# Right sides in 64x64 tiles with a block-diagonal state of two heads, moved by four transfers

## What is computed

```python
k = l2norm(silu(x @ Wk)); q = silu(x @ Wq); v = silu(x @ Wv)
beta = sigmoid(x @ Wbeta) * 2.0; log_f = log_sigmoid(x @ Wf1 @ Wf2)
# per step, two updates of the state S[b, h, key, value]:
bS = einsum('bhk,bhkv->bhv', b_t, S)
S = exp(g)[..., None] * S + a_t[..., None] * bS[:, :, None, :] + k_t[..., None] * v_t[:, :, None, :]
o = einsum('bhk,bhkv->bhv', q_t, S)
# then: y = rms_norm_per_head(o * sigmoid(gate)) * norm_w @ Wo
# x = layernorm(x + y); x = layernorm(x + x @ (W + lora).T + b)
```

## Time and profile before

| | us |
|---|---|
| median of 3 runs | 2623.15 (2622.76 to 2631.74) |
| span of the profiled execution, first to last instruction | 2622.0 |
| TensorE matmul busy | 2288.4 (87%) |
| TensorE weight load busy | 1721.9 (66%) |
| VectorE busy | 1601.7 (61%) |
| ScalarE busy | 1618.0 (62%) |
| GpSimd busy | 458.8 (17%) |
| matmuls of right_sides (L733), busy | 362.2 |
| mean granted clock of TensorE | 0.950 |

### The profile page before, as it was taken

One profiled execution on the slowest core, in us unless ns is written; L12 is line 12 of the kernel. 1 busy time (PEld: TensorE's weight loads), 2 busy tenths in 40 slices (PEclk: granted clock), 3 DMA queues, 4 the chain that ended last, 5 costly groups with the idle time before them and its releaser, 6 DMA issues.

```text
span 2622.0 us, 225147 instructions
## 1 busy us (share of the span) xinstructions
PE 2288.4 (87%) x102472; PEld 1721.9 (66%) x102472; DVE 1601.7 (61%) x3940; ACT 1618.0 (62%) x3048; POOL 458.8 (17%) x555
## 2 busy tenths in 40 slices
PE   6788898999988899998999998989999988999785
PEld 2556666666666666666676666666666666766573
DVE  2456366666556676656666665666666566666533
ACT  3556466666666666656666666666666666666543
POOL 1011111111111111111111111111111111111210
PEclk7879899999999999999999999999999999999987
DMA  3244455534555554455554455555445555534541
GB/s 95 74 110 121 110 148 148 141 104 127 145 141 151 137 141 111 132 138 146 144 137 118 124 145 146 148 141 142 113 129 143 145 148 148 136 103 132 140 125 41
DMA packets 692934, 338.90 MB, mean 129 GB/s; under 512 B 551794, under 2 KB 651728, under 8 KB 692816
## 3 DMA queue, kind: packets, MB, share of 16 engines
q1 hardware_dynamic: 692816, 337.67, 48.2%
HBM read 35.57 MB, written 16.78 MB: 20 GB/s over the span
## 4 chain that ended last, share of the span: by engine, by line
PE 86%; issue 10%; DVE 2%; ACT 1%; DMA 1%; SPq 0%; ACTq 0%; DVEq 0%
PE bank L570 14%; PE bank L733 13%; PE bank L712 11%; PE bank L704 8%; PE bank L724 7%; PE bank L716 5%; PE bank L593 5%; PE bank L683 5%; PE bank L622 5%; PE bank L643 3%; PE bank L577 3%; PE bank L694 2%; PE bank L602 2%; PE bank L587 2%; PE bank L584 2%
## 5 line engine op out<-in xcount | busy, mean ns | idle before, releaser
L473 POOL TENSOR_TENSOR state<-moved,edge 128x512 f32<-128x512 f32 x252 | 292.3, 1160 | 1821.9 <-DVE moved L1093 1821.9
L712 PE MATMUL bank<-parts,w_now 32*32 32x64 f32 x16512 | 420.1, 223 | 4.8 <-DMA w_now<-w_row 3.6
L570 PE MATMUL bank<-x_col,w_kqv 128*128 128x512 f32 x768 | 370.6, 619 | 48.5 <-issue 47.9
L856 ACT ACTIVATE parts<-bank,cf 128x256 f32<-128x256 f32 x512 | 214.6, 470 | 319.5 <-DVE o_col L1087 310.7
L716 PE MATMUL bank<-aq_now,delta 32*32 32x16 f32 x16512 | 403.7, 179 | 9.2 <-issue 9.2
L716 PEld LDWEIGHTS bank<-aq_now,delta 32*32 32x32 f32 x16512 | 391.7, 110 | 6.7 <-issue 6.7
L712 PEld LDWEIGHTS bank<-parts,w_now 32*32 32x32 f32 x16512 | 377.2, 110 | 17.1 <-issue 5.0
L733 PE MATMUL bank<-uq_now,s_now 32*32 32x24 f32 x32768 | 362.2, 189 | 14.5 <-issue 14.4
L733 PEld LDWEIGHTS bank<-uq_now,s_now 32*32 32x32 f32 x32768 | 337.1, 107 | 24.1 <-issue 18.2
L1116 DVE COPY_PREDICATED aq<-ci,bank 128x128 f32<-128x128 int32 x256 | 77.1, 301 | 410.3 <-PE bank L704 276.7
L1087 DVE TENSOR_TENSOR o_col<-qs,bank 128x64 f32<-128x64 f32 x512 | 89.5, 216 | 388.6 <-PE bank L716 384.7
(11 more groups left out here) (99 smaller groups left out, 3814.1 us busy)
## 6 DMA issues: line engine op xcount, KB each, us to landing
s_now<-state SPq DMA_DIRECT2D x256, 256.0 KB
uq_now<-uqv SPq DMA_DIRECT2D x256, 192.0 KB
t_now<-t_t SPq DMA_DIRECT2D x256, 128.0 KB, 2.0
w_now<-w_row SPq DMA_DIRECT2D x256, 128.0 KB
uq_a<-uqv SPq DMA_DIRECT2D x64, 384.0 KB
low<-uqv SPq DMA_DIRECT2D x64, 384.0 KB
x_col<-in_xt_dram SPq DMA_DIRECT2D x32, 512.0 KB, 5.8
w_a<-w_col SPq DMA_DIRECT2D x64, 256.0 KB
```

The source lines that it names most:

```text
L473: pool.tensor_tensor(state[:, qc, :, :, :].rearrange("p m b v -> p (m b) v"), moved[m % 2][:, :, :, :].rearrange("p m b v -> p (m b) v"), ...
L570: mm = pe.matmul(ps[:, :], w_kqv[:, a, w, f * P:(f + 1) * P], x_col[:, a, :], start=a == 0, stop=a == KT - 1)
L712: pe.matmul(ds_bank[quarter(h), m, :, :].rearrange("p b v -> p (b v)"), w_now[quarter(h), m, :], parts[quarter(h), m, :, :].rearrange("p b ...
L856: act.activation(parts[:, :, b, :], p2_bank, ACT.Copy, scale=cf[:, C_TAKE + b:C_TAKE + b + 1])
```

## The change

`state`, `moved` and `s_now` get the value index outside and the tile-and-sequence index (CT * GB = 16) inside. `s_now` is twice as wide: on each pair of heads (64 partitions) it holds a 64x64 block with the two heads' states on its diagonal and zeros beside them, for each of the 16. The zeros are set once at the start. `stage_first` fills it with four DMAs of 32 partitions each instead of one of 128, and the semaphore `s_in` counts four times as fast (register `turn64`). `right_sides` has 32 matmuls of 64x64 tiles in place of 64 of 32x32; its stationary operand is read with a step of 16 elements (64 bytes). VectorE's addition into `moved` reads `ds_bank` with a step of 32 elements, and GpSimd's decay broadcasts along the outer index. To make room, `prod` moves into the memory of `uq_a[0]`.

```diff
--- before.py
+++ after.py
@@ -151,7 +151,6 @@
         low = sb("low", [P, ROWS, HPH, ROWS])
         inv = sb("inv", [P, ROWS, HPH, ROWS])
         both = sb("both", [P, ROWS, HPH, GB, ROWS])
-        prod = sb("prod", [P, 2, 256])
         t_t = sb("t_t", [P, TILES, HD])
         edge = [sb(f"edge{c}", [P, LEN, PAIRS, HF, GB]) for c in range(2)]
         tail = sb("tail", [P, HF, GB, PAIRS])
@@ -160,15 +159,16 @@
             "p i h j -> p (i h j)")[:, 0:PAIR * QI * HF * UQ].rearrange("p (q c) -> p q c", c=HF * UQ)]
         w_a = [sb("w_a", [P, PAIR * CT, HD]), inv.rearrange(
             "p i h j -> p (i h j)")[:, 0:PAIR * CT * HD].rearrange("p (m c) -> p m c", c=HD)]
+        prod = uq_a[0].rearrange("p q c -> p (q c)")[:, 0:512].rearrange("p (a c) -> p a c", a=2)
         uq_now = sb("uq_now", [P, QI, HF * UQ])
-        s_now = sb("s_now", [P, CT, GB, HD])
+        s_now = sb("s_now", [P, 2 * HD, CT * GB])
         t_now = sb("t_now", [P, CT, HD])
         w_now = sb("w_now", [P, CT, HD])
         parts = sb("parts", [P, CT, GB, HD])
         aq_now = sb("aq_now", [P, CT, GB * TB])
 
-        state = sb("state", [P, QC, CT, GB, HD])
-        moved = [sb(f"moved{c}", [P, CT, GB, HD]) for c in range(2)]
+        state = sb("state", [P, QC, HD, CT * GB])
+        moved = [sb(f"moved{c}", [P, HD, CT * GB]) for c in range(2)]
         x_now = sb("x_now", [P, CT, HD])
         delta = sb("delta", [P, CT, HD])
         qs = [sb(f"qs{c}", [P, CT, GB, TB]) for c in range(4)]
@@ -242,7 +242,7 @@
         inv_spread = signal("inv_spread", GB)
         solve_step = signal("solve_step", 2 * (ROWS - 1))
         uq_in = signal("uq_in", 16 * CH)
-        s_in = signal("s_in", 16 * CH)
+        s_in = signal("s_in", 16 * HPH * CH)
         t_in = signal("t_in", 16 * CH, primed=16)
         aq_in = signal("aq_in", 16 * CH, primed=32)
         w_in = signal("w_in", 16 * CH, primed=32)
@@ -267,7 +267,7 @@
         rstd_ready = [signal(f"rstd{n}_ready", 1) for n in range(2)]
         shift_ready = [signal(f"shift{n}_ready", 1) for n in range(2)]
         h_normed = [signal(f"h{n}_normed", TT) for n in range(2)]
-        N_SET_UP = 13
+        N_SET_UP = 14
 
         def quarter(h):
             return slice(h * HD, (h + 1) * HD)
@@ -358,7 +358,9 @@
             def stage_first(c, n):
 
                 sp.dma_start(uq_now[:, :, :], of_chunks(uqv[c][:, :, 0:HF * UQ], n)).then_inc(uq_in.handle, 16)
-                sp.dma_start(s_now[:, :, :, :], state[:, n % QC, :, :, :]).then_inc(s_in.handle, 16)
+                for h in range(HPH):
+                    side = slice(h % 2 * HD, (h % 2 + 1) * HD)
+                    sp.dma_start(s_now[quarter(h), side, :], state[quarter(h), n % QC, :, :]).then_inc(s_in.handle, 16)
 
             def iteration(j, c):
                 for n in range(CH):
@@ -447,7 +449,7 @@
         def _(pool):
 
             until = pool.alloc_register("until")
-            for zeroed in (dd[:, :, :, :], both[:, :, :, :, :], aq[0][:, :, :], aq[1][:, :, :], state[:, :, :, :, :], t_now[:, :, :],
+            for zeroed in (dd[:, :, :, :], both[:, :, :, :, :], aq[0][:, :, :], aq[1][:, :, :], state[:, :, :, :], s_now[:, :, :], t_now[:, :, :],
                            w_now[:, :, :], parts[:, :, :, :], aq_now[:, :, :], x_now[:, :, :], delta[:, :, :], carry[:, :, 0:1]):
                 pool.memset(zeroed, 0.0).then_inc(set_up.handle, 1)
             for s in primed_signals:
@@ -470,9 +472,8 @@
                     pool.wait_ge(edge_ready.handle, edge_ready.at(g + 1, HF))
                 pool.wait_ge(s_added.handle, s_added.at(g, m + 1))
                 decay = edge[own][:, blk, qc * QI:(qc + 1) * QI, :, :].rearrange("p q f b -> p (q f b)")
-                pool.tensor_tensor(state[:, qc, :, :, :].rearrange("p m b v -> p (m b) v"),
-                                   moved[m % 2][:, :, :, :].rearrange("p m b v -> p (m b) v"),
-                                   decay.unsqueeze(2).to_broadcast([P, CT * GB, HD]),
+                pool.tensor_tensor(state[:, qc, :, :], moved[m % 2][:, :, :],
+                                   decay.unsqueeze(1).to_broadcast([P, HD, CT * GB]),
                                    ALU.mult).then_inc(state_ready.handle, 1)
 
             def iteration(j, c):
@@ -522,6 +523,7 @@
 
             turn = pe.alloc_register("turn")
             turn16 = pe.alloc_register("turn16")
+            turn64 = pe.alloc_register("turn64")
             part = pe.alloc_register("part")
             staged = pe.alloc_register("staged")
             freed = pe.alloc_register("freed")
@@ -729,9 +731,10 @@
 
                 for m in range(CT):
                     for b in range(GB):
-                        for h in range(HPH):
-                            mm = pe.matmul(p1_bank[quarter(h), m, b, :], s_now[quarter(h), m, b, :],
-                                           uq_of(uq_now, m % HF)[quarter(h), m // HF, b * RQ:(b + 1) * RQ],
+                        for i in range(HPH // 2):
+                            two = slice(i * 2 * HD, (i + 1) * 2 * HD)
+                            mm = pe.matmul(p1_bank[two, m, b, :], s_now[two, :, m * GB + b],
+                                           uq_of(uq_now, m % HF)[two, m // HF, b * RQ:(b + 1) * RQ],
                                            start=True, stop=True)
                 mm.then_inc(p1_filled.handle, 1)
 
@@ -752,11 +755,12 @@
 
                 pe.wait_ge(set_up.handle, N_SET_UP)
                 pe.wait_ge(uq_in.handle, turn16)
-                pe.wait_ge(s_in.handle, turn16)
+                pe.wait_ge(s_in.handle, turn64)
                 pe.wait_ge(qs_copied.handle, turn)
                 right_sides()
                 pe.reg_add(turn, turn, 1)
                 pe.reg_add(turn16, turn16, 16)
+                pe.reg_add(turn64, turn64, 64)
                 pe.reg_mov(part, s)
 
                 def some(lo, hi, work=dense):
@@ -817,6 +821,7 @@
             pe.reg_mov(opened, 0)
             pe.reg_mov(turn, 1)
             pe.reg_mov(turn16, 16)
+            pe.reg_mov(turn64, 64)
             pe.reg_mov(staged, a_staged[0].at(1, 32))
             pe.reg_mov(freed, low_copied.at(1, 0))
             for j in range(0, 2):
@@ -1075,7 +1080,7 @@
                 m, own = (n - 2, c) if n >= 2 else (CH + n - 2, 1 - c)
                 g = j if n >= 2 else j - 1
                 qc, blk = m % QC, m // QC
-                mine = state[:, qc, :, :, :]
+                mine = state[:, qc, :, :]
                 dve.wait_ge(p3_filled.handle, p3_filled.at(j, n + 1))
                 if m == 0 and there(g - 1):
                     dve.wait_ge(y_ready.handle, y_ready.at(g - 1, 1))
@@ -1090,7 +1095,8 @@
                     dve.wait_ge(s_added.handle, s_added.at(g, m - 1))
                 else:
                     dve.wait_ge(state_ready.handle, state_ready.at(g, m - 1))
-                dve.tensor_tensor(moved[m % 2][:, :, :, :], mine, ds_bank, ALU.add).then_inc(s_added.handle, 1)
+                dve.tensor_tensor(moved[m % 2][:, :, :], mine, ds_bank.rearrange("p m b v -> p v (m b)"),
+                                  ALU.add).then_inc(s_added.handle, 1)
 
             def turn_right_sides(j, c, n):
 
```

## The result

The changed kernel takes 3396.0 us (median of 4 runs, 3391.0 to 3398.5) against 2625.9 for the kernel before: a ratio of 1.2934, 95% interval 1.2894 to 1.2974. The forecast was 2700, its range ended at 3045.

A forecast was written before the change was run, and what follows sets the result against it. TensorE's string of stages was taken as the bound. Per slot 0.52 + 0.05 - 0.32 = +0.25 us, x 256 = +64; 2622.0 + 64 + 11 (half-clock slots) + 3 (transfers) gave 2700 us, range 2655 to 3045.

The forecast's parts named there:

- What bounds the kernel: Whole kernel: a string of TensorE stages, busy 87% of 2622.0 us; a slot's gain or loss reaches the end.
- The load blocks a tile by its columns: right_sides: weight columns set the pace, 27.3 ns a record; block 1.72 us against 1.20, +0.52 us a slot.
- The pause gives back 0.32 us: Pause before the dense stage: sequencer runs 14 records ahead, hiding part of the branches, -0.32 us a slot.
- the third rival: Pause before the dense stage: lead twice or more, pause falls from 0.82 to about 0.14 us; 2605 us, chance 7%.
- The switch of tile size costs 0.05: Before right_sides: new switch from 32x32 to 64x64 tiles costs 0 to 0.09 us, taken as +0.05 a slot.
- s_now by four transfers, +3 us: SyncE's queue: four issues delay s_now in one slot of eight, 0 to 19 us in all, taken as +3.
- moved with a step of 32 elements, at most 0.6 us more: VectorE's addition into moved: 0.68 us stays or becomes at most 1.3, with nothing on the path.
- The step of the weights costs nothing: right_sides' weight loads: reading s_now with 64 bytes between columns adds no time, as the 2700 us forecast assumed.
- the half-clock row: right_sides at half clock: 13.4 ns a record, 53.4 per tile, read as two cycles per weight column.
- a rival of 4%: More slots at half the clock, or s_now late in several slots: 2720 to 2850 us, chance 4%.
- the rival with the step: right_sides' weight loads: 64-byte step costs a factor of 1.9, block 3.26 us; 3006 us, chance 27%.
- The extra term for half-clock slots (+11): About one right_sides block in 20 at half clock costs 0.85 us more: 13 x 0.85 = +11 us.

The follow-up runs named there:

- e1: Changed kernel with its 64x64 tiles and four transfers, but the tile-and-sequence index outside, so the 64 weight columns are contiguous: 2769.2 us, ratio 1.0571.
- e6: Kernel before, with s_now moved by four transfers of 32 partitions instead of one, nothing else: 2648.3 us, ratio 1.0088.
- e5: Changed kernel, but each matmul of right_sides streams up to 96 moving columns instead of 24: 3057.5 us, ratio 1.1663.
- e9: Changed kernel with contiguous weights in its 64x64 tiles and up to 56 moving columns instead of 24: 2684.5 us, ratio 1.0239.

## Why the prediction was wrong

- *What bounds the kernel:* right. What TensorE's stages grew came through, less what the pauses gave back: 979.5 us more busy time (3267.9 against 2288.4) made the span 774.6 us longer. The list of waits ahead of the forecast was short of three that happen once or twice in the run (13.5 us for h_row, 12.8 for uq_a, 8.6 for cf); they are there after the change too, at 13.7, 13.1 and 8.8.
- *The load blocks a tile by its columns:* right in kind. e1 has 29.1 ns a record against 27.3 forecast and bounds of 26.7 to 30.4, a block of 1.84 us against 1.72.
- *The pause gives back 0.32 us:* 0.44 in e1: its last start at 1332.17 + 2.05 - 0.21 = 1334.01 leaves 0.64 us to L697, where it was 1.08. At 29.1 ns that lead is (0.44 + 0.06) / 0.029 = 17 records, the upper end of the reading. In the change itself the pause is 1009.98 - (1006.35 + 3.44) = 0.19 us, all but the switch, as the rival had it. The doubled lead of the third rival is out: 28 records at 29.1 ns would have left e1 a pause of 1.08 - (0.81 - 0.06) = 0.33 us here.
- *The switch of tile size costs 0.05:* nothing that shows. From deltas to right_sides 2.27 us pass in e1 (1329.90 to 1332.17) and 2.24 in the change, against 2.26 before; the waits ahead cover it.
- *s_now by four transfers, +3 us:* mis-sized, 26 us in e6. Two things failed: an issue of 32 partitions costs as much as one of 128 (I had put it between half and whole), and of what is queued behind it I named the next group's loads and gave them no price, where 12.9 of the 26 us show. In the change the longer slots hide most of it again (4.4 us).
- *moved with a step of 32 elements, at most 0.6 us more:* nothing at all, 681 ns against 680. What a step cost ScalarE in the earlier trace rows says nothing of VectorE. GpSimd's decay did get longer, 1273 ns against 1047 by its median, and TensorE's 4.4 us for s_now are all that it could have cost.
- *The step of the weights costs nothing:* **this is the step that failed**, the assumption under the 2700. I gave the rival 27%, at 3006 us with a factor of 1.9 and a block of 3.26 us, 3045 at a factor of two; its mechanism and the factor of two (3.44 us) are what happened, and e5, where the clock is held, came in at 3057. That ScalarE's factor came so near is luck, for VectorE's addition with the same step paid nothing. Against it I had set that a load takes one column in two cycles and may leave time for a longer access. The trace after refutes just that: the strided load takes the same 109 ns a tile at either clock. At half of it the contiguous load of e1 takes nearly as long (52.9 ns a record against 54.6), so the step is all but free there, and the half-clock row that I leaned on could not have shown its cost at the full clock. What sets the strided pace is open.
- *The clock:* the range failed here. I had it as a rival of 4% with 2720 to 2850 us, added to the forecast and not to the rival with the step. But the two go together: a block that is three times as long with the same columns streams a third, and 339 us came on top. The extra term for half-clock slots (+11) was sized by the share of before, as though the change could not move that share. In e1 already, 2769 against e9's 2684, 85 us came with the clock (0.927 against 0.977).

## What to carry to other kernels

Fewer matmul instructions are worth only what the instructions bound: read the pace from start to start at both clocks, compare it with the loaded and the streamed columns of a tile, and price a merge of tiles by the columns that each tile has to load. Lay the stationary operand out so that its columns lie at most 8 bytes apart; with 16 and with 64 bytes the fp32 load took twice as long here in 64x64 tiles, and with 64 bytes in 32x32 tiles too. Where a change makes a TensorE stage longer without streaming more, add the clock of the stages behind it to every rival, not only to the forecast.

## What the runs showed of the hardware that I had not expected

- A strided fp32 weight load ran at 54.6 ns a record of 64 columns in two tiles at a granted clock of 1.00 and of 0.50 alike. The contiguous one follows the clock: a block of e1 at half of it, from its timeline and by windows (clock 0.50), takes 3.61 - 0.28 = 3.33 us, 52.9 ns a record against 29.1.

```profile
1221.26 3.61 PE L737 MATMUL bank<-uq_now,s_now 64*64 64x24 f32 x64
```

```profile
1221.30:1224.50 3.20, 3.20 (x65) 3.20 (x62) 0.95 (x3) 1.11 (x3) 1.05 (x1) 0.50 0.27 61
```

- TensorE fell to 1.2 GHz while it was busy without a gap: after blocks of 3.44 us with 24 moving columns a record the next stage ran at 0.51, and with 96 columns in the same blocks the mean clock was 0.971 instead of 0.823. Streaming columns that nobody needs made the kernel before 0.6% faster.
- One DMA issue took about 0.64 us for 32 partitions as for 128.
